# The last stage's output product in f16 halves: high and low parts of the mean, with the low part left in PSUM by a negated identity

## The chip, the cores and the metric

One Trainium2 chip, one NeuronCore. The metric is the device time of one execution of the program, in microseconds; of the kernel before, three runs are at hand. The shares of a stage come from one profiled execution.

## The reference

A graph network of two residual layers over 50,000 nodes with 256 features and 75,000 edges, sorted by destination. What the change touches is the end of the second layer, an attention over each node's edges with 8 heads:

```python
h = jnp.maximum(_layernorm(x, axis=-1), 0.0)
q = (h @ Wq + bq).reshape(n, DH, H) * scaling
k = (h @ Wk + bk).reshape(n, DH, H)
v = (h @ Wv + bv).reshape(n, DH, H)
s = jnp.einsum('edh,edh->eh', q[row], k[col])
m = jax.ops.segment_max(s, row, num_segments=n)
e = jnp.exp(s - m[row])
a = e / jax.ops.segment_sum(e, row, num_segments=n)[row]
out = jax.ops.segment_sum(a[:, None, :] * v[col], row, num_segments=n)
x = x + out.reshape(n, -1) @ Wo + bo
```

## The kernel before

The nodes stand in 98 tiles of 512 (128 partitions, 4 rows of nodes each: ROWS). The program runs through five parts, one after the other, which hand on tables in HBM and a few constants in SBUF: a preparation (weights, edges; line 388 and on), stage A (first layer's norm and product), stage B (second product and the sort of the edges), stage C (sums of neighbours, second norm, q, k and v; here v is written by `evacuate`, L1781, from a product in f16 parts at L1691), and stage E, the attention and the output product. The change is in stage E, with some constants made ready in the preparation and at the start of stage C.

Stage E is a pipeline written out by hand (`over_ring`): in one step every engine works on several tiles at once, `at(l)` being the tile that entered l steps ago. Six steps make one turn of a loop, so that a ring of six buffers has fixed addresses. Each engine has its own list for a step, taken strictly in order, and waits on semaphores:

- TensorE (`step` at L2180): turns the one-hot matrix of tile 0 (L2186) and counts its prefix (L2190); first half of the output product of tile 4 (`product`, L2154); first half of the mean of tile 3 (`mean(at(3), 0)`, L2166: four transposes, L2172, and the neighbours' share added, L2176); second half of the output product of tile 4; the edges' attention of tile 2 (L2202); second half of the mean of tile 3; q by edge for tile 0 (L2214); the scores laid out by node for tile 1 (L2223, into `e_small_ps`).
- VectorE (`step` at L2397): from that layout of tile 2 it masks (`e_seen`, L2328), takes peaks and differences, and while ScalarE takes the exponential does the products with k of tile 1 (L2344) and adds half a tile of output to x (`result`, L2314); then the attention of tile 2 is normalised (`e_attention`, L2360). It ends the step with scores, ranks, `e_of_edge` (L2391, which reads the same bank as L2223 writes) and the other half of `result`.
- ScalarE: copies (L2093 to L2102), the exponential (L2107), then for each of the two halves (kc) of the features a copy of the mean of tile 3 from PSUM (`e_mean_t`, L2118) and scalings of tile 2 by its attention (`e_mine`, L2126): 16 after the first copy and 8 after the second.
- GpSimd: scales the neighbours' v (L2065) and gathers rows (L2073).

The output product is in f32 and has, for each of 4 rows of a tile, one bf16 product for the bias (L2160) and two f32 products (L2162), each of which the profile shows as two MATMUL instructions:

```python
pe.wait_ge(mean_t_ready, t * 2 + 2)
for j in range(2):
    row = half * 2 + j
    nc.tensor.matmul(out_ps[:, j, :], all_b[:, :], b_out[:, :], start=True, stop=False)
    for kc in range(KC):
        last = nc.tensor.matmul(out_ps[:, j, :], mean_t[u][:, kc, row * P:(row + 1) * P],
                                w_out[:, kc, :], start=False, stop=kc == KC - 1)
```

## Time and profile before

| | us |
|---|---|
| median of 3 runs | 3436.98 |
| lowest and highest | 3434.53, 3438.17 |
| the profiled execution, its time | 3437.03 |
| the profiled execution, its span | 3435.2 |

The span is from the first to the last instruction of the trace. PE is TensorE's matmuls, PEld its weight loads (they run beside matmuls), DVE VectorE, ACT ScalarE, POOL GpSimd. A matmul's duration in the trace is longer than the distance to the next one's start, since matmuls are pipelined: rates are read from the starts. An idle time in brackets at the end of a timeline's row stands before that row, with what released it.

### The profile page before, as it was taken

To read this page: it belongs to the slowest core of one execution; us is meant where nothing else is said; L and a number is where in the kernel's file an instruction comes from. 1 tells how busy PE (TensorE), PEld (TensorE's weight loads), DVE (VectorE), ACT (ScalarE), POOL (GpSimd) and SP (SyncE) were. 2 spreads that over 40 slices of the span, in tenths; PEclk is the share of its full clock that TensorE was granted. 3 is DMA by queue.
4 is the path that set the end of the run, shared out by engine and by line. 5 is a ranking of instruction groups with operands and counts; after the bars stand their busy time and mean duration, and the time that the engine had idled before them with its cause. 6 is when DMAs were issued, how large, how long until landed. Compare 5 with 4: busy or idle time off the path is not lost. (4 is left out here: it accounts for less than half of the span.)

```text
span 3435.2 us, 80786 instructions
## 1 busy us (share of the span) xinstructions
PE 3089.9 (90%) x20244; PEld 2502.0 (73%) x20244; DVE 2812.0 (82%) x7373; ACT 2503.3 (73%) x7074; POOL 1953.9 (57%) x1668
## 2 busy tenths in 40 slices
PE   1699999699999569999999999994999999999999
PEld 0355555477776448888888888883899999999998
DVE  8788888578888358888888888885888888888887
ACT  0588888599997847777777777762777777777776
POOL 0344444045555277777777777763555555555553
PEclk6799999899999869999999999996999999999999
DMA  1355555388887658888888888875677777777774
GB/s 35 132 205 203 202 202 202 142 301 306 306 307 254 255 196 309 309 313 304 313 308 309 306 311 310 306 273 190 234 250 258 257 256 250 254 254 257 256 248 144
DMA packets 335629, 861.22 MB, mean 251 GB/s; under 512 B 98483, under 2 KB 152922, under 8 KB 323018
## 3 DMA queue, kind: packets, MB, share of 16 engines
q1 hardware_dynamic: 241082, 678.75, 55.2%
q0 software_dynamic: 66256, 78.94, 7.9%
q10 hardware_dynamic: 28224, 102.77, 7.4%
q8 instruction: 25, 0.41, 0.0%
q14 instruction: 42, 0.34, 0.0%
HBM read 521.95 MB, written 416.52 MB: 273 GB/s over the span
## 5 line engine op out<-in xcount | busy, mean ns | idle before, releaser
L1691 PE MATMUL c_qkv_ps<-w_qkv_hi,c_ht_hi 128*128 128x256 f16 x2352 | 642.0, 273 | 0.0
L1691 PE MATMUL c_qkv_ps<-w_qkv_lo,c_ht_hi 128*128 128x256 f16 x2352 | 642.0, 273 | 0.0
L1691 PE MATMUL c_qkv_ps<-w_qkv_hi,c_ht_lo 128*128 128x256 f16 x2352 | 642.0, 273 | 0.0
L2126 ACT ACTIVATE e_mine<-e_mine,e_attention 128x32 f32<-128x32 f32 x2352 | 518.7, 307 | 70.3 <-DVE e_attention L2360 70.3
L2073 POOL DMA_INDIRECT e_kv<-kv_table,e_near x392 | 402.1, 1026 | 113.1 <-issue 98.8
L1561 POOL DMA_INDIRECT c_got<-y_table,c_near x392 | 395.1, 1008 | 108.9 <-issue 98.0
L2162 PE MATMUL e_out_ps<-w_out,e_mean_t 128*128 128x256 f32 x1568 | 392.8, 380 | 0.0
L792 POOL DMA_INDIRECT dst_slots<-dst_word,dst_goal x240 | 236.9, 987 | 267.7 <-ACT a_hn L828 190.3
L862 PE MATMUL a_h_ps<-a_ht,w_t 128*128 128x512 f32 x784 | 361.1, 603 | 25.1 <-ACT h L810 21.5
L2065 POOL TENSOR_TENSOR e_kv<-e_kv,e_part_of 128x1024 f32<-128x1024 f32 x98 | 187.1, 1909 | 342.4 <-DVE e_part_of L2395 342.3
L1331 POOL DMA_INDIRECT src_slots<-staged_word,staged_goal x240 | 233.3, 972 | 250.8 <-DVE sort_lane_hot L1220 177.5
L1122 PE MATMUL mix_ps<-w_mix,hb 128*128 128x256 f32 x1568 | 358.0, 382 | 17.4 <-ACT hb L1091 17.4
L1122 PEld LDWEIGHTS mix_ps<-w_mix,hb 128*128 128x128 f32 x1568 | 296.9, 191 | 63.9 <-ACT hb L1091 21.5
L1554 POOL TENSOR_TENSOR c_x<-c_agg,c_x 128x1024 f32<-128x1024 f32 x98 | 231.2, 2359 | 127.6 <-ACT c_agg L1608 115.8
L2162 PEld LDWEIGHTS e_out_ps<-w_out,e_mean_t 128*128 128x128 f32 x1568 | 267.4, 191 | 44.0
L1678 PE MATMUL c_sum_ps<-c_got,c_sum_hot 128*128 128x256 f32 x784 | 218.8, 403 | 72.2 <-DVE c_agg L1802 48.1
L862 PEld LDWEIGHTS a_h_ps<-a_ht,w_t 128*128 128x128 f32 x784 | 141.6, 190 | 187.9 <-issue 187.9
L1619 ACT ACTIVATE c_hn<-c_x,c_shift,c_rstd 128x256 f32<-128x256 f32 x392 | 203.5, 590 | 95.7 <-DVE c_shift L1823 95.7
L1546 POOL TENSOR_TENSOR c_qk<-c_q,c_kv 128x1024 f32<-128x1024 f32 x98 | 232.5, 2373 | 34.8 <-DVE c_kv L1787 32.6
L1691 PEld LDWEIGHTS c_qkv_ps<-w_qkv_lo,c_ht_hi 128*128 128x128 f16 x2352 | 230.5, 98 | 27.0
L1691 PEld LDWEIGHTS c_qkv_ps<-w_qkv_hi,c_ht_lo 128*128 128x128 f16 x2352 | 230.5, 98 | 26.9
L1691 PEld LDWEIGHTS c_qkv_ps<-w_qkv_hi,c_ht_hi 128*128 128x128 f16 x2352 | 230.5, 98 | 24.7
(432 smaller groups left out, 7682.2 us busy)
## 6 DMA issues: line engine op xcount, KB each, us to landing
kv_table<-c_kv SPq DMA_DIRECT2D x98, 1024.0 KB, 6.7
h_table<-h ACTq DMA_DIRECT2D x98, 512.0 KB
h<-h_table SPq DMA_DIRECT2D x98, 512.0 KB
y_table<-y_out ACTq DMA_DIRECT2D x98, 512.0 KB
agg_table<-agg_out SPq DMA_DIRECT2D x98, 512.0 KB, 3.2
c_agg<-agg_table SPq DMA_DIRECT2D x98, 512.0 KB, 5.6
x_table<-c_x SPq DMA_DIRECT2D x98, 512.0 KB, 2.9
q_table<-c_q SPq DMA_DIRECT2D x98, 512.0 KB, 4.3
```

The costliest lines, as they stand in the source:

```text
L792: nc.gpsimd.indirect_dma_start(out=dst_slots, out_offset=bass.IndirectOffsetOnAxis(ap=dst_goal[:, k:k + 1], axis=0), in_=dst_word[:, k:k + ...
L862: last = nc.tensor.matmul(h1_ps[:, oc * TILE:(oc + 1) * TILE], w1_t[:, kc, oc * P:(oc + 1) * P], ht[u][:, kc, :], start=kc == 0, stop=kc = ...
L1122: last = nc.tensor.matmul(mix_ps[u][:, j * D:(j + 1) * D], hb[u][:, kc, j * P:(j + 1) * P], w_mix[:, kc, :], start=kc == 0, stop=kc == KC - 1)
L1331: nc.gpsimd.indirect_dma_start(out=src_slots, out_offset=bass.IndirectOffsetOnAxis(ap=staged_goal[h][:, k:k + 1], axis=0), in_=staged_word ...
L1546: nc.gpsimd.tensor_tensor(qk[u][:, :, :], qb[w][:, :, :], kv[w][:, :, 0, :], ALU.mult).then_inc(qk_ready, 1)
L1554: nc.gpsimd.tensor_tensor(x1[u][:, :, :], agg[w][:, :, :], xb[w][:, :, :], ALU.add).then_inc(x1_ready, 1)
L1561: nc.gpsimd.indirect_dma_start(out=got[w][:, j, :], out_offset=None, in_=y_table, in_offset=bass.IndirectOffsetOnAxis(ap=near[w][:, j:j + ...
L1678: last = nc.tensor.matmul(sum_ps[:, j * D:(j + 1) * D], sum_hot[w][:, row, :], got[w][:, row, :], start=True, stop=True)
L1691: last = nc.tensor.matmul(qkv_ps[n][:, j * D:(j + 1) * D], h[u][:, kc, j * P:(j + 1) * P], wt[:, kc, n * D:(n + 1) * D], start=m == 0, sto ...
L2073: nc.gpsimd.indirect_dma_start(out=kv[w][:, j, :], out_offset=None, in_=kv_table, in_offset=bass.IndirectOffsetOnAxis(ap=near[w][:, j:j + ...
L2126: last = nc.scalar.activation(of_head, of_head, ACT.Copy, scale=attention[u][:, j, h, 0:1])
L2162: last = nc.tensor.matmul(out_ps[:, j, :], mean_t[u][:, kc, row * P:(row + 1) * P], w_out[:, kc, :], start=False, stop=kc == KC - 1)
```

## The change

Stage E's output product takes f16 parts. The mean of tile 3 is copied by ScalarE from PSUM to f16 (`mean_hi`); TensorE adds to the same PSUM bank the product of a negated identity with `mean_hi` (`rest`), so that the bank holds what the f16 copy lacks; ScalarE copies that to f16 (`mean_lo`). The output product is then, for each half of the features, hi by hi, hi by lo and lo by hi, six f16 products in place of two f32 ones. The weights of the output are split once; they and v are scaled by powers of two, which `result` takes back.

```diff
@@ ScalarE, stage E
-                            nc.scalar.activation(mean_t[u][:, kc, :], mean_ps[kc][:, :], ACT.Copy).then_inc(mean_t_ready, 1)
+                            nc.scalar.activation(mean_hi[u][:, kc, :], mean_ps[kc][:, :], ACT.Copy).then_inc(mean_hi_ready, 1)
                         if at(2) is not None:
...
                             last.then_inc(own_shared, 1)
+                        if at(3) is not None:
+                            t, u = ring_tile(at(3)), at(3)[1] % 2
+                            act.wait_ge(rest_ready, t * 2 + (kc + 1))
+                            nc.scalar.activation(mean_lo[u][:, kc, :], mean_ps[kc][:, :], ACT.Copy).then_inc(mean_lo_ready, 1)
@@ TensorE, stage E
-                    pe.wait_ge(mean_t_ready, t * 2 + 2)
+                    pe.wait_ge(mean_lo_ready, t * 2 + 2)
...
-                        for kc in range(KC):
-                            last = nc.tensor.matmul(out_ps[:, j, :], mean_t[u][:, kc, row * P:(row + 1) * P],
-                                                    w_out[:, kc, :], start=False, stop=kc == KC - 1)
+                        passes = [(m, w, kc) for kc in range(KC)
+                                  for m, w in ((mean_hi, w_out_hi), (mean_hi, w_out_lo), (mean_lo, w_out_hi))]
+                        for k, (m, w, kc) in enumerate(passes):
+                            last = nc.tensor.matmul(out_ps[:, j, :], m[u][:, kc, row * P:(row + 1) * P],
+                                                    w[:, kc, :], start=False, stop=k == len(passes) - 1)
...
+                def rest(at, kc):
+                    t, u = ring_tile(at), at[1] % 2
+                    pe.wait_ge(mean_hi_ready, t * 2 + (kc + 1))
+                    nc.tensor.matmul(mean_ps[kc][:, :], minus_h[:, :], mean_hi[u][:, kc, :], start=False, stop=True,
+                                     skip_group_check=True).then_inc(rest_ready, 1)
...
                     if at(4) is not None:
                         product(at(4), 1)
+                    if at(3) is not None:
+                        rest(at(3), 0)
...
                             last.then_inc(q_ready, 1)
+                    if at(3) is not None:
+                        rest(at(3), 1)
                     if at(1) is not None:
@@ VectorE, stage E
-                    v.tensor_tensor(here, out_ps[:, :, :], here, ALU.add).then_inc(result_ready, 1)
+                    v.scalar_tensor_tensor(here, out_ps[:, :, :], out_unscale[:, 0:1], here, ALU.mult, ALU.add).then_inc(result_ready, 1)
@@ VectorE, stage C
-                    v.scalar_tensor_tensor(goes, qkv_ps[n][:, :].rearrange("p (j d) -> p j d", j=ROWS), unscale[:, 0:1],
+                    v.scalar_tensor_tensor(goes, qkv_ps[n][:, :].rearrange("p (j d) -> p j d", j=ROWS), (unscale_v if n == 2 else unscale)[:, 0:1],
@@ VectorE, start of stage C (before it: in the preparation, without the scaling by both_scale and the split of w_out)
+                v.tensor_scalar(b_out_n[:, :], b_out_n[:, :], both_scale[:, 0:1], None, ALU.mult)
+                chain(v.tensor_scalar(w_flat, w_flat, out_scale[:, 0:1], None, ALU.mult))
+                chain(v.tensor_copy(w_out_hi[:, :, :], w_out[:, :, :]))
+                chain(v.tensor_tensor(w_out_lo[:, :, :], w_out[:, :, :], w_out_hi[:, :, :], ALU.subtract))
...
@@ GpSimd, preparation
+                    pool.memset(minus_h[:, :], 0.0).then_inc(raising, 1)
+                    pool.wait_ge(raising, 3)
+                    pool.affine_select(out=minus_h[:, :], in_=minus_h[:, :], compare_op=ALU.not_equal, fill=-1.0, base=0,
+                                       pattern=[[-1, P]], channel_multiplier=1).then_inc(const_ready, 1)
...
+                    pool.wait_ge(o_peak_ready, 1)
+                    pool.partition_all_reduce(o_peaks[:, :], o_peak[:, :], P, bass.bass_isa.ReduceOp.max).then_inc(o_peaks_ready, 1)
```

In the preparation VectorE also takes the largest exponents of the output weights and of v's bias (three passes over 512 and two over 256 elements a partition) and makes the scales from them, some ten operations on one element a partition; the seven operations that split the output's bias into three bf16 rows move from there to the start of stage C. One semaphore of stage B, `agg_stored`, is now cleared with the others of its part.

The order of TensorE's work about the end of a step of stage E, in the kernel before (`e_mean_ps` is the mean of tile 3, `e_q_ps` q by edge, `e_small_ps` the scores laid out, `e_out_ps` the output product):

```order
L2176 MATMUL e_mean_ps<-e_hot,e_kv 128x128 x4
L2214 MATMUL e_q_ps<-e_q,e_hot_t 128x256 x4
L2223 MATMUL e_small_ps<-e_layered,e_hot 128x64 x4
L2186 MATMUL e_turn_ps<-ident_h,e_hot_h 128x128 x4
L2190 MATMUL e_prefix_ps<-e_hot_h,raised_h 128x128 x4
L2160 MATMUL e_out_ps<-b_out,all_b 128x256
L2162 MATMUL e_out_ps<-w_out,e_mean_t 128x256 x2
```

and after the change, at the same place:

```order
L2236 MATMUL e_mean_ps<-e_hot,e_kv 128x128 x4
L1389 ISA
L2276 MATMUL e_q_ps<-e_q,e_hot_t 128x256 x4
L2223 MATMUL e_mean_ps<-e_mean_hi,minus_h 128x512
L2287 MATMUL e_small_ps<-e_layered,e_hot 128x64 x4
L2243 REGISTER_ALU
L2246 MATMUL e_turn_ps<-ident_h,e_hot_h 128x128 x4
L2250 MATMUL e_prefix_ps<-e_hot_h,raised_h 128x128 x4
L2212 MATMUL e_out_ps<-b_out,all_b 128x256
L2216 MATMUL e_out_ps<-w_out_hi,e_mean_hi 128x256
L2216 MATMUL e_out_ps<-w_out_lo,e_mean_hi 128x256
```

One product over 512 columns, from `e_mean_hi`, stands between q and the layout of the scores.

ScalarE, from the first of the two copies of the mean to the end of the step, before:

```order
L2118 ACTIVATE e_mean_t<-e_mean_ps 128x512
L2126 ACTIVATE e_mine<-e_mine,e_attention 128x32 x16
L2117 REGISTER_ALU
L2118 ACTIVATE e_mean_t<-e_mean_ps 128x512
L2126 ACTIVATE e_mine<-e_mine,e_attention 128x32 x8
```

and after:

```order
L2166 ACTIVATE e_mean_hi<-e_mean_ps 128x512
L2174 ACTIVATE e_mine<-e_mine,e_attention 128x32 x16
L2179 ACTIVATE e_mean_lo<-e_mean_ps 128x512
L2165 REGISTER_ALU
L2166 ACTIVATE e_mean_hi<-e_mean_ps 128x512
L2174 ACTIVATE e_mine<-e_mine,e_attention 128x32 x8
L2179 ACTIVATE e_mean_lo<-e_mean_ps 128x512
```

The copy of the low part of the first half stands between the 16 scalings and the copy of the second half; the low part of the second half ends the step.

## Rows read from the trace of the kernel before

**Rows 1.** The page of the profile, busy time of each engine.

```profile
PE 3089.9 (90%) x20244; PEld 2502.0 (73%) x20244; DVE 2812.0 (82%) x7373; ACT 2503.3 (73%) x7074; POOL 1953.9 (57%) x1668
```

**Rows 2.** Busy time by window: stages C and E; PE, PEld, DVE, ACT, POOL, clock.

```profile
1400.00:2370.00 970.00, 907.62 (x7439) 789.62 (x7436) 818.06 (x1788) 684.21 (x1831) 719.40 (x489) 0.99 0.81 299
2428.00:3379.00 951.00, 950.99 (x6916) 867.26 (x6915) 849.66 (x1728) 727.02 (x2818) 547.13 (x455) 1.00 0.74 254
```

**Rows 3.** Groups by line, PE, window 2428:3379 (xcount | busy us, mean ns).

```profile
L2162 PE MATMUL e_out_ps<-w_out,e_mean_t 128*128 128x256 f32 x1456 | 364.7, 380 | 0.0
```

**Rows 4.** Timeline of PE, one step of stage E (start us, us, engine, line).

```profile
3002.99 1.00 PE L2223 MATMUL e_small_ps<-e_layered,e_hot 128*128 128x64 f32 x8
3003.83 0.39 PE L2186 MATMUL e_turn_ps<-ident_h,e_hot_h 128*128 128x128 f16 x4
...
3004.28 0.27 PE L2160 MATMUL e_out_ps<-b_out,all_b 128*128 128x256 bf16 x1
3004.38 1.03 PE L2162 MATMUL e_out_ps<-w_out,e_mean_t 128*128 128x256 f32 x4
3005.25 0.27 PE L2160 MATMUL e_out_ps<-b_out,all_b 128*128 128x256 bf16 x1
```

**Rows 5.** Timeline of DVE, the same step and the start of the next.

```profile
3004.17 0.42 DVE L2328 TENSOR_TENSOR e_seen<-e_small_ps,absent 128x256 f32<-128x256 f32 x1 [0.39 <-PE e_small_ps L2223]
...
3008.65 0.46 DVE L2360 TENSOR_TENSOR e_attention<-e_weight,e_inverse 128x288 f32<-128x288 f32 x1 [0.19 <-DVE e_inverse L2355]
...
3012.99 0.41 DVE L2391 TENSOR_TENSOR e_of_edge<-e_small_ps,e_layer 128x256 f32<-128x256 f32 x1
...
3014.80 0.42 DVE L2328 TENSOR_TENSOR e_seen<-e_small_ps,absent 128x256 f32<-128x256 f32 x1 [0.34 <-PE e_small_ps L2223]
```

**Rows 6.** Timeline of ACT, the same step.

```profile
3007.76 0.60 ACT L2118 ACTIVATE e_mean_t<-e_mean_ps 128x512 f32<-128x512 f32 x1 [1.39 <-PE e_mean_ps L2176]
3009.14 3.50 ACT L2126 ACTIVATE e_mine<-e_mine,e_attention 128x32 f32<-128x32 f32 x16 [0.79 <-DVE e_attention L2360]
3012.55 0.57 ACT L2118 ACTIVATE e_mean_t<-e_mean_ps 128x512 f32<-128x512 f32 x1
3013.03 1.80 ACT L2126 ACTIVATE e_mine<-e_mine,e_attention 128x32 f32<-128x32 f32 x8
```

**Rows 7.** Timelines of PE and DVE, a step that ends no turn of six.

```profile
2982.16 1.00 PE L2223 MATMUL e_small_ps<-e_layered,e_hot 128*128 128x64 f32 x8
...
2983.30 0.42 DVE L2328 TENSOR_TENSOR e_seen<-e_small_ps,absent 128x256 f32<-128x256 f32 x1 [0.46 <-PE e_small_ps L2223]
...
2987.69 0.46 DVE L2360 TENSOR_TENSOR e_attention<-e_weight,e_inverse 128x288 f32<-128x288 f32 x1 [0.19 <-DVE e_inverse L2355]
...
2991.77 0.42 DVE L2391 TENSOR_TENSOR e_of_edge<-e_small_ps,e_layer 128x256 f32<-128x256 f32 x1
```

**Rows 8.** Timelines of ACT and PE at the drain of stage E.

```profile
3409.39 0.57 ACT L2118 ACTIVATE e_mean_t<-e_mean_ps 128x512 f32<-128x512 f32 x1
...
3410.02 0.28 PE L2160 MATMUL e_out_ps<-b_out,all_b 128*128 128x256 bf16 x1 [0.29 <-ACT e_mean_t L2118]
```

**Rows 9.** One line of DVE: duration ns min/median/max, first and last start.

```profile
L2328 DVE TENSOR_TENSOR e_seen<-e_small_ps,absent x98: 423/425/425, 2398.4 to 3409.8; 128x256 f32<-128x256 f32 x98
```

**Rows 10.** Timeline of ACT in stage C, the copy to f16.

```profile
1395.24 0.58 ACT L1585 ACTIVATE c_ht_hi<-c_turn_ps 128x512 f16<-128x512 f32 x1
1395.71 0.71 ACT L1627 ACTIVATE c_sum_hot<-c_sum_hot,one_col 127x512 f32<-127x512 f32 x1
```

**Rows 11.** Timelines of DVE: start, end of preparation, start of stage C.

```profile
8.03 0.77 DVE L530 CAST edges_f<-edges 128x1176 f32<-128x1176 int32 x1 [8.03 <-POOL far_end L471]
...
90.44 0.28 DVE L669 CAST b_thirds<-b_out_n 128x256 bf16<-128x256 f32 x1
...
93.70 0.15 DVE L677 TENSOR_SCALAR unscale<-w_peaks 128x1 f32<-128x1 f32 x1
...
1224.15 0.69 DVE L1802 TENSOR_TENSOR c_agg<-c_sum_ps,c_agg 128x512 f32<-128x512 f32 x1 [15.55 <-PE c_sum_ps L1678]
```

More of the change, by code:

```diff
@@ L272, in build @@
         unscale = sb("unscale", [P, 1], where=early)
+        unscale_v = sb("unscale_v", [P, 1], where=early)
+        out_scale = sb("out_scale", [P, 1], where=early)
+        both_scale = sb("both_scale", [P, 1], where=early)
+        w_out = sb("w_out", [P, KC, D], where=early)
+        b_out_n = sb("b_out_n", [P, D], where=early)
         b_qkv = sb("b_qkv", [P, 3 * D], where=early)
@@ L383, in build @@
             n_loads = 14 + H
-            b_out_n = sb("b_out_n", [P, D], where=part)
-            b_rest = sb("b_rest", [P, 2, D], where=part)
-            b_thirds = sb("b_thirds", [P, 3, D], BF16, where=part)
+            o_power = sb("o_power", [P, KC * D], I32, where=part)
+            o_peak = sb("o_peak", [P, 1], where=part)
+            o_peaks = sb("o_peaks", [P, 1], where=part)
+            v_bias = sb("v_bias", [P, D], I32, where=part)
+            v_peak = sb("v_peak", [P, 1], where=part)
+            v_unscale = sb("v_unscale", [P, 1], where=part)
+            v_scale = sb("v_scale", [P, 1], where=part)
+            o_unscale = sb("o_unscale", [P, 1], where=part)
+            o_peak_ready = sem("o_peak_ready")
+            o_peaks_ready = sem("o_peaks_ready")
             with nc.Block() as block:
@@ L665, in _ @@
                     v.tensor_scalar(dst_goal[:, :], pair_f[:, 0, :], -float(subtiles), float(1 << 21), ALU.add, ALU.min)
-                    left = b_out_n[:, :]
-                    for third in range(3):
-                        link(v.tensor_copy(b_thirds[:, third, :], left))
-                        if third < 2:
-                            link(v.tensor_tensor(b_rest[:, third, :], left, b_thirds[:, third, :], ALU.subtract))
-                            left = b_rest[:, third, :]
-                    link(v.tensor_scalar(b_out[:, :], b_thirds[:, 0, :], ident[:, 0:1], None, ALU.mult))
-                    for third in (1, 2):
-                        link(v.scalar_tensor_tensor(b_out[:, :], b_thirds[:, third, :], ident[:, third:third + 1], b_out[:, :], ALU.mult, ALU.add))
                     dve.wait_ge(w_peaks_ready, 1)
@@ L971, in build @@
             y_stored = [sem(f"y_stored{u}") for u in two]
-            agg_stored = [pool_dma_sem(f"agg_stored{u}") for u in two]
+            agg_stored = [sem(f"agg_stored{u}") for u in two]
             own_scale = sb("own_scale", [P, NT * ROWS], where=part)
@@ L1459, in build @@
             not_slow = sb("c_not_slow", [P, 1], where=part)
+            b_rest = sb("b_rest", [P, 2, D], where=part)
+            b_thirds = sb("b_thirds", [P, 3, D], BF16, where=part)
             slots_loaded = sem("c_slots_loaded")
@@ L1777, in _ @@
                 v.scalar_tensor_tensor(slot_node[:, :], vacant[:, :], float(FAR), slots_f[:, 1, :], ALU.mult, ALU.add)
+                w_flat = w_out[:, :, :].rearrange("p k n -> p (k n)")
+                v.tensor_scalar(b_out_n[:, :], b_out_n[:, :], both_scale[:, 0:1], None, ALU.mult)
+                chain(v.tensor_scalar(w_flat, w_flat, out_scale[:, 0:1], None, ALU.mult))
+                chain(v.tensor_copy(w_out_hi[:, :, :], w_out[:, :, :]))
+                chain(v.tensor_tensor(w_out_lo[:, :, :], w_out[:, :, :], w_out_hi[:, :, :], ALU.subtract))
+                left = b_out_n[:, :]
+                for third in range(3):
+                    chain(v.tensor_copy(b_thirds[:, third, :], left))
+                    if third < 2:
+                        chain(v.tensor_tensor(b_rest[:, third, :], left, b_thirds[:, third, :], ALU.subtract))
+                        left = b_rest[:, third, :]
+                chain(v.tensor_scalar(b_out[:, :], b_thirds[:, 0, :], ident[:, 0:1], None, ALU.mult))
+                for third in (1, 2):
+                    chain(v.scalar_tensor_tensor(b_out[:, :], b_thirds[:, third, :], ident[:, third:third + 1], b_out[:, :], ALU.mult, ALU.add))
                 for l in range(LAYERS):
@@ L1931, in build @@
             part_of = [sb(f"e_part_of{w}", [P, ROWS, H], where=part) for w in short]
-            mean_t = [sb(f"e_mean_t{u}", [P, KC, TILE], where=part) for u in two]
+            mean_hi = [sb(f"e_mean_hi{u}", [P, KC, TILE], F16, where=part) for u in two]
+            mean_lo = [sb(f"e_mean_lo{u}", [P, KC, TILE], F16, where=part) for u in two]
             turn_ps = part.enter_context(nc.psum_tensor("e_turn_ps", [P, ROWS, 2 * P], F16))
```

31 lines of the change are left out of this document (26 added, 5 removed).

## The prediction

> **What bounds the kernel now.** The page first: PE is busy 90% of the span, VectorE 82%, ScalarE 73% [rows 1]. That is a mean over stages, so the busy times by window come next. From 2428 to 3379 us, in stage E, PE is busy for all of 951 us at a granted clock of 1.00 (2.4 GHz), its weight loads for 867, VectorE for 850, ScalarE for 727 [rows 2]. That stretch holds 1456 instructions of L2162 [rows 3], 16 to a tile, so 91 tiles; from tile to tile e_seen starts (3409.8 - 2398.4) / 97 = 10.43 us apart [rows 9]. Per tile VectorE works 9.3 us and ScalarE 8.0. The reader is to see two things in the timelines of one step. PE's rows follow each other without idle time [rows 4], while VectorE has 0.34 to 0.46 us of idle time before e_seen, released by PE [rows 5, 7], and ScalarE waits 1.39 us for the mean and 0.79 for the attention [rows 6]. So PE sets the pace, but VectorE's slack is small: in a step that ends a turn of six, from e_seen to e_seen are 10.63 us [rows 5], in which PE's L2223 waits for e_of_edge, since both use one bank.
>
> **What the change takes from PE.** A row of nodes now costs from L2160 to the next L2160 3005.25 - 3004.28 = 0.97 us [rows 4]. A product over 256 columns in 16 bits takes the distance from L2160 to L2162, 0.10 to 0.11 us; I take 0.109. With seven of them a row is 0.76, and four rows save 0.84 us per tile. The two new products over 512 columns cost twice that distance each, 0.22, so 0.44 for both. PE's work falls by 0.40 us, to about 10.05. Here lies the gain that the change could have, and it is hidden unless nothing else closes the circle first.
>
> **What it adds on ScalarE.** Two more copies of 128x512 from PSUM. Such a copy takes ScalarE 0.48 us until its next instruction starts, 3013.03 - 3012.55 [rows 6], and 0.57 us until it is done. One to f16 took the same in stage C, 0.58 with the next one 0.47 later [rows 10]. ScalarE's work rises to 8.0 + 0.96 = 9.0 us per tile, well below 10.4: by its sum there is room. What counts is the place: the first new copy stands behind the 16 scalings, ahead of the copy that `rest(at(3), 1)` on PE waits for, and behind that one on PE stands L2223, which VectorE waits for.
>
> **The circle that this closes.** The attention of tile 2 needs the scores that L2223 wrote at the end of the step before. The scalings need that attention, the copies stand behind the scalings, the new product needs the copy, and the next L2223 stands behind the product. All of it is within one step, so its length is a floor under the step. From the end of L2223 (3002.99 + 1.00) [rows 4] in order: to e_seen 0.18; to the end of e_attention, 3009.11 - 3004.17 = 4.94 [rows 5]; to the first scaling 0.03; sixteen scalings 3012.55 - 3009.14 = 3.41; the low copy of the first half 0.48; the high copy of the second half, to its end, 0.57 [rows 6]; from a copy's end to PE, 3410.02 - 3409.96 = 0.06 [rows 8]; the new product 0.22; L2223 to its end 1.00 [rows 4]. The sum is 10.89 us. In a step that ends no turn, the first two terms are 0.14 and 2988.15 - 2983.30 = 4.85 [rows 7], and the sum is 10.76. Five of the one to one of the other give 10.78. None of the terms has slack inside: VectorE's idle times in that stretch are the 0.19 before e_attention, which follow from its own chain.
>
> I take 10.84. Between VectorE and PE a wait is followed by 0.14 to 0.18 us [rows 5, 7] where ScalarE to PE took 0.06; the circle has new waits on both engines, and the difference of about 0.1 may be paid at one of them. With none of it paid, 10.76; with two paid in full, 11.0.
>
> A second circle goes over two steps. From the end of L2223 to the end of the high copy of the second half as above, but only 0.48 of it, then eight scalings (8 times 3.41 / 16 = 1.70), the low copy 0.57, and 0.06 to PE: 0.15 + 4.87 + 0.03 + 3.41 + 0.48 + 0.48 + 1.70 + 0.57 + 0.06 = 11.75 to the start of the output product. From there PE has its step but for the first two rows and L2223: 10.43 - 0.45 (3004.28 - 3003.83) - 0.84 (3003.83 - 3002.99) [rows 4] = 9.14, less 0.84, plus 0.22 for the first new product, and then 0.22 and 1.00. That is 21.5 us for two steps, 10.75 for one: just below the first circle, so PE will stand twice in a step, about 0.6 us before the output product and about 0.2 before the second new product.
>
> **The rest of the change.** `result` has an operation with one more multiplication on VectorE, with the same sizes; L2344, of that kind, ran between the same kinds of operands at the pace of `result`: nothing. In the preparation VectorE loses the 3.26 us of the bias's split (93.70 - 90.44) [rows 11] and gets five short passes and some ten operations of 0.15 each, which I price between 2.5 and 4: -1 to +1. GpSimd makes one more constant ahead of VectorE's first instruction, which waits for GpSimd until 8.03 [rows 11]: two small operations, under 1 us. Together +0.5. At the start of stage C VectorE gets the split and three passes over the weights, 5 to 6 us in all; the cover is its 15.55 us of idle time before the first c_agg, released by PE [rows 11]. Were that gone, 5 us would be added. In the drain, the last three tiles' output products wait for the copy already, as in the step of [rows 8]; a product and a copy more, 0.22 + 0.57 and what lies between, less two halves of the product that are 0.42 shorter: +1.
>
> **Sum.** 97 steps times (10.84 - 10.43) = +40, +0.5 and +1: +41.5 us on the profiled execution's 3437.03, so 3478.5. That execution is 0.05 us from the median of the three runs, so the median after is put at 3478 us. Slower or faster by less than 0.2% (7 us) is what a measurement of this kernel cannot tell from no change.
>
> **Rivals.**
>
> PE lightened and nothing in its way. If the low copy or the scalings cost the circle at least 0.6 us less than summed (the point from which this decides is a circle under 10.2), the floor is VectorE's: e_seen to the end of e_of_edge 2992.19 - 2983.30 = 8.89 [rows 7], 0.15 to PE, 1.00 for L2223, 0.14 back, 10.18; at the end of a turn 10.63 as now. The mean of 10.26 saves 0.17 times 97, 16 us: 3422 us. For it speaks that PE is the engine without idle time in [rows 2] and ScalarE has 2.4 us free; against it, that every term of the circle is a row. The Trainium skill, Perfetto Trace Analysis, "Identifying the Most-Contended Engine", says to find the engine with the highest occupancy and optimize it first. By that rule the change, which takes 0.40 us per tile from PE and adds to an engine with room, would end here, at a gain; the trace agrees that PE is the busiest and does not show that lightening it is paid out. 9%.
>
> The waits add up. The circle of two steps is within 0.1 us of the first. If PE comes late to the output product and the mean of the next half is then late for ScalarE as well, the two no longer overlap; half of the 0.6 us wait, paid on top of 0.41, would be +0.3 per tile more, 3508 us; a tenth to a half of it gives 3484 to 3508. 12%.
>
> The clock. PE gets idle times. In stage C it was busy 908 of 970 us at a granted clock of 0.99 [rows 2], and here it would be busy 10.05 of 10.84, 93%, in gaps under 1 us. The Trainium skill, TensorE: Matmul & The Clock Gate, "A second HAM failure mode: psum-queue depth-cycling", tells of a kernel whose short idles between groups of matmuls made the clock go to and fro. Should it fall to 1.2 GHz for a tenth of the stage, PE's 10.05 would become 20.1 there, and 9.7 steps of 9.3 us more give +90: 3570 us. 2%.
>
> No difference that can be measured: the circle is 0.3 shorter than summed, between the two. 4%.
>
> **How the numbers follow.** The forecast, a floor of 10.70 to 11.0 and so 3465 to 3493 us, has 73%. Faster by over 0.2% has the first rival's 9%, no difference 4%, slower the forecast, the added waits and the clock: 87%. The range leaves out the faster rival, the clock and the far half of the added waits: 3463 to 3500 us.
>
> **What would show it.** In the changed kernel's trace the distance of e_seen should be 10.75 to 10.95 us; PE should show idle time before the output product's L2160, released by ScalarE's low copy, and before the second product from e_mean_hi, released by the high copy; PE's busy share in stage E about 93% at a clock of 1.00; VectorE's idle time before e_seen 0.8 us or more. The prediction is wrong if PE has no idle time there, if a scaling starts later than 0.1 us after e_attention, or if e_attention itself is late because `result` or the exponential waits.

## The result, and the profile after

| | before | after |
|---|---|---|
| median, us | 3437.47 (4 runs of the same session) | 3483.81 (4 runs, 3481.78 to 3485.63) |
| the profiled execution, its span | 3435.2 | 3480.0 |
| ratio | | 1.0134, 95% interval 1.0120 to 1.0149 |

The change makes the kernel 46.3 us slower; the forecast was 3478 us and a range of 3463 to 3500. The profiled execution of after took 3481.78 us.

Busy time of each engine on the page, and further down the chain that ended last:

```profile
PE 3080.6 (89%) x21224; PEld 2477.8 (71%) x21224; DVE 2828.7 (81%) x7392; ACT 2583.4 (74%) x7270; POOL 1956.9 (56%) x1671
...
PE 12%; ACT 10%; DVE 7%; issue 3%; DVEq 0%; DMA 0%; POOL 0%; ACTq 0%; POOLq 0%
```

That chain is followed back from the last instruction, in shares of the span, and covers about a third of it. In the kernel before it lay on PE almost alone; now it passes through three engines:

```profile
PE 30%; DMA 1%; DVE 1%; issue 0%; ACT 0%; POOL 0%; POOLq 0%; SPq 0%; DVEq 0%; ACTq 0%
```

Busy time by window in stage E (PE, PEld, DVE, ACT, POOL, clock), the answer to [rows 2]:

```profile
2440.00:3390.00 950.00, 903.59 (x7503) 809.25 (x7502) 826.46 (x1658) 767.43 (x2873) 524.60 (x437) 1.00 0.71 244
```

PE is no longer busy all the time: 46 of 950 us are idle, at a granted clock of 1.00 as before. No engine is busy throughout, which points to a circle of waits. The busy shares of the page hide this, since 89% stands where 90% stood [rows 1].

The waits in stage E (idle engine, who released it: us in total, times, longest), window 2450 to 3400:

```profile
ACT e_mean_hi L2166 <- PE e_mean_ps L2236: 134.6, 87, 1.6
...
DVE e_seen L2392 <- PE e_small_ps L2287: 61.2, 87, 0.8
...
ACT e_mine L2174 <- DVE e_attention L2424: 46.3, 87, 0.6
PE e_out_ps L2212 <- ACT e_mean_lo L2179: 43.4, 88, 0.5
PEld e_mean_ps L2223 <- ACT e_mean_hi L2166: 38.1, 87, 0.5
```

Both waits that the prediction named on PE are there, once a step each: 0.5 us before the output product (L2212), released by the low copy (about 0.6 forecast), and 0.4 us in the weight load of the second new product (L2223), released by the high copy (about 0.2 forecast).

One step in three timelines (line numbers have moved: the layout of the scores, L2223 before, is L2287 now, and L2223 is the new product). VectorE:

```profile
3004.73 0.42 DVE L2392 TENSOR_TENSOR e_seen<-e_small_ps,absent 128x256 f32<-128x256 f32 x1 [0.76 <-PE e_small_ps L2287]
...
3007.28 0.75 DVE L2378 SCALAR_TENSOR_TENSOR e_x<-e_out_ps,out_unscale,e_x 128x512 f32<-128x512 f32 x1
...
3009.22 0.46 DVE L2424 TENSOR_TENSOR e_attention<-e_weight,e_inverse 128x288 f32<-128x288 f32 x1 [0.19 <-DVE e_inverse L2419]
...
3015.60 0.42 DVE L2392 TENSOR_TENSOR e_seen<-e_small_ps,absent 128x256 f32<-128x256 f32 x1 [0.78 <-PE e_small_ps L2287]
```

ScalarE:

```profile
3009.71 3.50 ACT L2174 ACTIVATE e_mine<-e_mine,e_attention 128x32 f32<-128x32 f32 x16 [0.51 <-DVE e_attention L2424]
3013.11 0.58 ACT L2179 ACTIVATE e_mean_lo<-e_mean_ps 128x512 f16<-128x512 f32 x1
3013.59 0.58 ACT L2166 ACTIVATE e_mean_hi<-e_mean_ps 128x512 f16<-128x512 f32 x1
```

PE:

```profile
3003.58 1.00 PE L2287 MATMUL e_small_ps<-e_layered,e_hot 128*128 128x64 f32 x8
...
3005.53 0.28 PE L2212 MATMUL e_out_ps<-b_out,all_b 128*128 128x256 bf16 x1 [0.50 <-ACT e_mean_lo L2179]
...
3008.40 0.27 PE L2212 MATMUL e_out_ps<-b_out,all_b 128*128 128x256 bf16 x1
...
3009.17 0.27 PE L2212 MATMUL e_out_ps<-b_out,all_b 128*128 128x256 bf16 x1
...
3014.23 0.39 PE L2223 MATMUL e_mean_ps<-e_mean_hi,minus_h 128*128 128x512 f16 x1
3014.45 1.00 PE L2287 MATMUL e_small_ps<-e_layered,e_hot 128*128 128x64 f32 x8
```

Read as the prediction's circle, from the end of L2287 at 3004.58: 0.15 to e_seen, 4.95 to the end of e_attention (3009.68), 0.03, scalings 3.40, low copy 0.48, high copy 0.58 to its end (3014.17), 0.06, new product 0.22, L2287 1.00. The sum is 10.87 us, and from e_seen to e_seen are 3015.60 - 3004.73 = 10.87. The circle has no slack: it is the step. This step ends no turn of six; the one that does takes 11.01 us, from 3026.50 to 3037.51. Both are 0.11 to 0.12 above the prediction's sums of 10.76 and 10.89.

Over the stage:

```profile
L2392 DVE TENSOR_TENSOR e_seen<-e_small_ps,absent x98: 423/424/426, 2394.5 to 3450.7; 128x256 f32<-128x256 f32 x98
```

(3450.7 - 2394.5) / 97 = 10.89 us a step, against 10.43 [rows 9]. Of the 44.8 us between the two spans, 44.8 lie between the first and the last e_seen (1056.2 - 1011.4); ahead of it after is 3.9 us earlier, and behind it 3.9 us longer.

### The profile page after: what moved, and what is told of

Same layout as the page of the kernel before. It is cut to its first block and busy times, and to the rows that moved or that the text cites. A ratio compares the mean times of both kernels' runs of the same rounds, so it can differ in the third digit from the quotient of the medians.

```text
span 3480.0 us, 83059 instructions
## 1 busy us (share of the span) xinstructions
PE 3080.6 (89%) x21224; PEld 2477.8 (71%) x21224; DVE 2828.7 (81%) x7392; ACT 2583.4 (74%) x7270; POOL 1956.9 (56%) x1671
## 5 line engine op out<-in xcount | busy, mean ns | idle before, releaser
L1592 POOL DMA_INDIRECT c_got<-y_table,c_near x392 | 402.2, 1026 | 108.4 <-issue 96.4
L1669 ACT ACTIVATE c_state<-c_raw,no_self,has_self 128x8 f32<-128x8 f32 x392 | 122.0, 381 | 155.8 <-DVE c_raw L1881 155.8
L857 ACT ACTIVATE a_hn<-a_x,a_shift,a_rstd 128x256 f32<-128x256 f32 x392 | 203.3, 589 | 45.1 <-DVE a_shift L193 45.1
```

The costliest lines, as they stand in the source:

```text
L1592: nc.gpsimd.indirect_dma_start(out=got[w][:, j, :], out_offset=None, in_=y_table, in_offset=bass.IndirectOffsetOnAxis(ap=near[w][:, j:j + ...
```

## Experiments

Three sets of four kernels. Times are compared with runs of the kernel before on the same chip. In the first and third sets it took 3437.8 and 3437.7 us, as here; in the second, on another chip, 3486.7 us.

| kernel | median, us | ratio to before, 95% | e_seen to e_seen, mean of 97, us |
|---|---|---|---|
| low0_later | 3482.80 | 1.0116 to 1.0147 | 10.863 |
| low1_sooner | 3480.15 | 1.0105 to 1.0136 | 10.851 |
| both_moved | 3440.82 | 1.0001 to 1.0020 | 10.494 |
| high_between | 3443.94 | 1.0009 to 1.0027 | 10.505 |
| plain_result | 3763.34 | 1.0774 to 1.0821 | 13.107 (other chip) |
| hi_only | 3675.54 | 1.0490 to 1.0555 | 12.412 (other chip) |
| before_two_copies | 3492.51 | 1.0007 to 1.0025 | 10.531 (other chip) |
| result_sooner | 3657.12 | 1.0482 to 1.0520 | 12.244 (other chip) |
| changed_again | 3485.49 | 1.0122 to 1.0153 | 10.873 |
| plain_result_2 | 3477.85 | 1.0098 to 1.0129 | 10.817 |
| hi_only_2 | 3477.34 | 1.0100 to 1.0131 | 10.864 |
| result_sooner_2 | 3441.38 | 1.0003 to 1.0021 | 10.471 |

The rival theories: ScalarE's added work costs by its sum; PE's wait for the low copy is the cost; PE's own work is the floor.

### low0_later: the first low copy out of the first circle

ScalarE's order for a step (high and low copies of the two halves, scalings):

```diff
-high 0, scalings 1-16, low 0, high 1, scalings 17-24, low 1
+high 0, scalings 1-16, high 1, low 0, scalings 17-24, low 1
```

> The changed kernel with ScalarE's low copy of the first half moved from ahead of the high copy of the second half to behind it; nothing else. Theory A (two circles, each a floor under the step): the first circle, from L2223 over e_seen, the attention, sixteen scalings and the two copies back to L2223, loses one copy's 0.48 us and falls from 10.89 to 10.41; the second, over two steps and the output product, keeps both copies and stands at about 10.75 to 10.84 per step. So the step shortens by 0.05 to 0.14 us and the time falls by 5 to 14 us from the changed kernel's, to 3470 to 3479 us, with PE's wait for the low copy before the output product as long as before or longer. Rival B (only the first circle counts): the step falls to the PE's or VectorE's own 10.4 and the time to 3437 us or below. Rival C (what counts is ScalarE's summed work, which is unchanged): 3484 us, no change.

Measured 3482.80 us, 1 us below after: theory A's gain of 5 to 14 us did not come, though 0.48 us left the first circle. Rival B is out; rival C, no change, fits this run alone. The timelines of PE, VectorE and ScalarE show what held the step:

```profile
3002.43 1.00 PE L2300 MATMUL e_small_ps<-e_layered,e_hot 128*128 128x64 f32 x8
...
3004.55 0.28 PE L2225 MATMUL e_out_ps<-b_out,all_b 128*128 128x256 bf16 x1 [0.68 <-ACT e_mean_lo L2172]
...
3013.29 1.00 PE L2300 MATMUL e_small_ps<-e_layered,e_hot 128*128 128x64 f32 x8
...
3015.42 0.28 PE L2225 MATMUL e_out_ps<-b_out,all_b 128*128 128x256 bf16 x1 [0.69 <-ACT e_mean_lo L2172]
```

```profile
3003.57 0.42 DVE L2405 TENSOR_TENSOR e_seen<-e_small_ps,absent 128x256 f32<-128x256 f32 x1 [0.57 <-PE e_small_ps L2300]
...
3004.90 1.28 DVE L2421 SCALAR_TENSOR_TENSOR e_qk<-e_q_ps,e_kv 128x512 f32<-128x512 f32 x2
3006.30 0.75 DVE L2391 SCALAR_TENSOR_TENSOR e_x<-e_out_ps,out_unscale,e_x 128x512 f32<-128x512 f32 x1
...
3008.24 0.46 DVE L2437 TENSOR_TENSOR e_attention<-e_weight,e_inverse 128x288 f32<-128x288 f32 x1 [0.19 <-DVE e_inverse L2432]
```

```profile
3008.73 3.50 ACT L2183 ACTIVATE e_mine<-e_mine,e_attention 128x32 f32<-128x32 f32 x16 [0.51 <-DVE e_attention L2437]
3012.14 0.57 ACT L2166 ACTIVATE e_mean_hi<-e_mean_ps 128x512 f16<-128x512 f32 x1
3012.62 0.57 ACT L2172 ACTIVATE e_mean_lo<-e_mean_ps 128x512 f16<-128x512 f32 x1
3013.09 1.79 ACT L2183 ACTIVATE e_mine<-e_mine,e_attention 128x32 f32<-128x32 f32 x8
3014.79 0.57 ACT L2172 ACTIVATE e_mean_lo<-e_mean_ps 128x512 f16<-128x512 f32 x1
```

The prediction's circle over two steps comes near, but has slack. From L2300's end at 3003.43 to the output product at 3015.42 are 11.99 us, and from the output product to the end of the next L2300, 3014.29 - 3004.55, 9.74; the prediction had 11.75 and 9.74. But 0.20 us of the 11.99 are a wait inside it: `result` (L2391) starts 1.40 us after the start of the two products with k, where 1.20 is the distance without a wait. Without it the two steps are 21.53, or 10.77 for one, and the step is 10.86.

What sets the step is a shorter circle, which the prediction did not have. It is closed within one step and does not pass through L2300: the output product of tile 4 is needed by `result`, which stands on VectorE ahead of the attention of tile 2; the scalings need that attention, all copies stand behind the first sixteen of them, and the next output product needs the last low copy. From the output product at 3004.55: 1.75 to `result`, 2.40 to the end of e_attention, 0.03, scalings 3.41, copies 0.48 and 0.47, scalings 1.70, the last low copy 0.57 to its end, 0.06 to the next output product. The sum is 10.87, which is the whole distance 3015.42 - 3004.55. The move of the first low copy leaves this circle as long as it was. In the changed kernel it is as long as the first one: from the output product to `result` are 1.75 us there too, and the output products of the steps at 3005.53 and 3016.40 are 10.87 apart. So two circles stand at the same length in the changed kernel, and low0_later cuts only one.

### low1_sooner: the second low copy ahead of the last scalings

```diff
-high 0, scalings 1-16, low 0, high 1, scalings 17-24, low 1
+high 0, scalings 1-16, low 0, high 1, low 1, scalings 17-24
```

> The changed kernel with ScalarE's low copy of the second half moved from behind the last eight scalings to ahead of them; nothing else. Theory A: this takes the eight scalings, 1.7 us, out of the circle over two steps and leaves the first circle, 10.89 us, as it is, so the distance between two e_seen stays 10.85 to 10.93 us and the time within 4 us of the changed kernel's 3484, while PE's wait before the output product (43.4 us over 88 steps) shrinks to nearly nothing and its wait before the second new product grows. Rival B (the wait for the low copy before the output product, about 0.5 us a step, is what the change costs): the time falls by 20 to 40 us. Rival C (ScalarE's sum): no change, and the waits stay where they are.

Measured 3480.15 us and 10.85 us a step, at the edge of A's 4 us: the first circle still stands. The waits, window 2450 to 3400:

```profile
DVE e_seen L2405 <- PE e_small_ps L2300: 61.6, 88, 0.8
PEld e_mean_ps L2236 <- ACT e_mean_hi L2166: 57.9, 88, 0.7
...
PE e_out_ps L2225 <- DVE e_x L2391: 23.3, 87, 0.3
```

The row "PE e_out_ps <- ACT e_mean_lo", 43.4 us in after, is gone, and 3.7 us of time went with it; the wait for the high copy grew from 38.1 to 57.9 instead. The circle through `result` lost 1.70 us, and the first circle alone holds the step. So PE's largest visible wait was by itself worth under 4 us, and rival B falls.

### both_moved: both circles cut

```diff
-high 0, scalings 1-16, low 0, high 1, scalings 17-24, low 1
+high 0, scalings 1-16, high 1, low 0, low 1, scalings 17-24
```

> The changed kernel with ScalarE's order: high copy of half one, sixteen scalings, high copy of half two, both low copies, eight scalings. Same instructions, same sums. Theory A: both circles are cut, the first to 10.41 us, the second below it, so the step is 10.41 to 10.48 us and the time 3436 to 3444 us: all of the change's loss is given back by the order alone. Rival C (ScalarE's added work or the two extra hand-overs cost what was lost, wherever they stand): 3475 to 3484 us. Rival D (PE is bound by its own work again): with PE at 10.05 a step it would be faster than the kernel before, 3400 to 3425 us; A says that this gain stays out.

Measured 3440.82 us: 43 of the 46 us are given back by the order of ScalarE's list, with every instruction of the change in place. Rival C falls with it. Either half alone gave 1 to 4 us, both together 43; that is what two circles of one length do. The step of 10.494 us is just above A's 10.41 to 10.48. Rival D falls too: PE's work is below the kernel before's and is not paid out. Busy time in stage E:

```profile
2440.00:3390.00 950.00, 924.11 (x7771) 839.21 (x7770) 857.57 (x1719) 806.91 (x2986) 536.83 (x447) 1.00 0.73 251
```

PE idles 26 us there, and every engine has room. PE's timeline of a step that ends a turn shows one wait, for the first half of `result`:

```profile
3001.72 1.02 PE L2300 MATMUL e_small_ps<-e_layered,e_hot 128*128 128x64 f32 x8
...
3006.34 0.28 PE L2225 MATMUL e_out_ps<-b_out,all_b 128*128 128x256 bf16 x1 [0.28 <-DVE e_x L2391]
```

### high_between: more slack in both circles

```diff
-high 0, scalings 1-16, high 1, low 0, low 1, scalings 17-24
+high 0, scalings 1-12, high 1, low 0, scalings 13-16, low 1, scalings 17-24
```

> The changed kernel with ScalarE's order: high copy of half one, twelve scalings, high copy of half two, low copy of half one, four scalings, low copy of half two, eight scalings. Same instructions. Theory A: four scalings, 0.85 us, and a copy, 0.48, are out of the first circle (9.56 us left); the circle over two steps comes to about 10.4, and VectorE's own floor is 10.2 in a step that ends no turn and 10.63 in one that does, 10.26 to 10.35 in the mean. So the step is 10.3 to 10.45 us and the time 3425 to 3440 us, equal to the kernel before or up to 12 us below it. Rival C (ScalarE's sum): 3475 to 3484 us. Rival D (PE's own 10.05 is the only floor left): 3400 us.

Measured 3443.94 us, 4 us above A's range, and 10.505 us a step, as in both_moved. A further 0.85 us off the first circle brings nothing, so another chain holds the step at 10.50, above the 10.26 that I had put as VectorE's floor. The wait in the row above gave the next candidate: L2300, e_seen, the products with k, `result`, the second half of the output product (one PSUM bank serves both halves), and PE's list on to L2300.

### result_sooner and result_sooner_2: that candidate cut

```diff
-products q times k 0 and 1, result 0
+product q times k 0, result 0, product q times k 1
```

> The kernel with the high copy of half two between the scalings, and in it VectorE's `result` of the first half moved from behind the second product q times k to between the two. Its reason: in both kernels with ScalarE's order changed the step is 10.50 us, not the 10.3 to 10.4 hoped for, and PE stands 0.28 us a step before the second half of the output product, released by `result`. That is a third circle: L2300's end, 0.15 to e_seen, 3.35 to the end of `result`, 0.06, then PE without idle time for 6.0 and L2300 again, 10.42 to 10.70. Theory A: the move takes 0.6 us out of it, and the step falls to VectorE's floor, 10.25 in a step that ends no turn and 10.65 to 10.70 in one that does, 10.33 in the mean; the time is 3420 to 3432 us, 6 to 17 us below the kernel before and about 16 below the run without the move. Rival (PE's wait for `result` is made up elsewhere, or another chain stands just below 10.5): 3438 to 3444 us.

> As in the first try, for a chip on which the step keeps its pace. Theory A: without the third circle the step is VectorE's floor, and the shortest steps of the first try, 10.34 and 10.42 in steps that end no turn, 10.56 and 10.67 at a turn, give 10.40 to 10.45 in the mean: 97 times 0.06 to 0.10 us, 6 to 10 us, below the runs without the move (3441 and 3444 us), so 3430 to 3437 us, equal to the kernel before or just below. Rival: 3440 to 3444 us, if PE's wait for `result` only moves on.

On the chip of the third set 3441.38 us, and 10.47 us a step against 10.49 and 10.51: 0.6 us out of that circle gave at most 0.03, and the rival is right. PE's timeline:

```profile
3004.80 1.08 PE L2301 MATMUL e_small_ps<-e_layered,e_hot 128*128 128x64 f32 x8
...
3011.11 1.10 PE L2278 MATMUL e_small_ps<-e_attention,e_hot_t 128*128 128x64 f32 x8 [0.19 <-DVE e_attention L2438]
...
3015.50 1.07 PE L2301 MATMUL e_small_ps<-e_layered,e_hot 128*128 128x64 f32 x8
```

PE's wait for `result` is gone, and it waits for e_attention instead: from L2301's end at 3005.88 to L2278 at 3011.11 are 5.23 us of VectorE's chain, and from there to L2301's end at 3016.57 5.46 us of PE's own list, together 10.69 in this step, which ends a turn. This further circle holds VectorE's chain and half of PE's list and nothing of ScalarE's copies. It is read from rows of one kind of step; no run cut it, so that it sets the pace is not shown. No version here beats the kernel before.

### plain_result and plain_result_2: the price of `result`

The kernel leaves out the scaling back of the output product:

```diff
-v.scalar_tensor_tensor(here, out_ps[:, :, :], out_unscale[:, 0:1], here, ALU.mult, ALU.add)
+v.tensor_tensor(here, out_ps[:, :, :], here, ALU.add)
```

> The changed kernel with `result` as the plain addition of the kernel before; it leaves out the scaling back of the output product by out_unscale. In the changed kernel's trace this operation takes 0.74 us, before it took 0.68, and it stands once inside the first circle, between e_seen and e_attention, which the prediction priced at nothing. Theory A: the first circle falls by 0.07 us, from 10.89 to 10.82, and the time by 97 times 0.07 = 7 us, to 3474 to 3480 us. Rival: `result` is hidden beside ScalarE's exponential and costs nothing: 3482 to 3485 us.

> As in the first try (the scaling back by out_unscale is left out), for a chip on which the step keeps its pace. Theory A: `result` at 0.68 instead of 0.74 us shortens the first circle by 0.07 us, steps of 10.82 instead of 10.89, and 4 to 9 us off the changed kernel of this set. Rival: nothing off. On a chip as in the set before, only the undisturbed steps can be read: 10.78 to 10.80 in a step that ends no turn, instead of 10.86.

VectorE's timeline in result_sooner_2 has two operations of one size side by side, a product with k, which multiplies by a constant and then by a tensor, and `result`, which multiplies by a factor per partition and then adds:

```profile
3007.47 0.68 DVE L2422 SCALAR_TENSOR_TENSOR e_qk<-e_q_ps,e_kv 128x512 f32<-128x512 f32 x1
3008.07 0.74 DVE L2392 SCALAR_TENSOR_TENSOR e_x<-e_out_ps,out_unscale,e_x 128x512 f32<-128x512 f32 x1
```

In the third set plain_result took 3477.85 us against 3485.49 of changed_again, 7.6 us less, and 10.817 against 10.873 us a step, 97 times 0.056 = 5.4 us of it in the steps. Theory A holds. That `result` takes longer than the product with k may come from the factor or from the second operation; no run separates them. The second set's run of it is told below.

### hi_only and hi_only_2: a third of the output product

The kernel leaves out the two passes with low parts:

```diff
-((mean_hi, w_out_hi), (mean_hi, w_out_lo), (mean_lo, w_out_hi))
+((mean_hi, w_out_hi),)
```

> The changed kernel with the output product's two passes by low parts left out, 16 of 24 products over 256 columns per tile, so its output has the high parts' product alone; both copies, both new products and all waits stay. PE's work falls by 16 times 0.109 = 1.75 us per tile, to about 8.3. Theory A (the first circle sets the step, and the output product is not in it): the distance between two e_seen stays 10.85 to 10.91 us and the time 3478 to 3486 us. Rival D (PE's work sets the pace, as its 95% busy share in stage E of the changed kernel would suggest): the step falls by up to 1.75 us to VectorE's floor near 10.3, time 3420 to 3440 us. Between them: if the circle over two steps were what binds, half of 1.75 would come off, and the next floor, the first circle, would stop it.

> As in the first try (two of three passes of the output product are left out), for a chip on which the step keeps its pace. Theory A: steps stay at 10.84 to 10.91 us and the time within 6 us of the changed kernel of this set. In the first try, on the slower chip, the shortest steps came in rows of 10.84 to 10.93 us with PE at its full pace, which already speaks for it. Rival D (PE's work counts): 3420 to 3440 us where the changed kernel takes 3484.

In the third set, with 1.75 us less of PE's work per tile:

```profile
2440.00:3390.00 950.00, 789.09 (x6104) 665.62 (x6103) 825.93 (x1660) 768.19 (x2875) 520.78 (x438) 1.00 0.71 244
```

and the row of e_seen (first and last start):

```profile
L2392 DVE TENSOR_TENSOR e_seen<-e_small_ps,absent x98: 423/425/426, 2394.8 to 3448.6; 128x256 f32<-128x256 f32 x98
```

PE is busy 83% instead of 95%, and the step stays (3448.6 - 2394.8) / 97 = 10.86 us. Removing 170 us of PE's work (97 times 1.75) took 8 us off the time (2 us outside A's bound of 6), of which 5 lie behind the last e_seen: 3475.5 - 3448.6 = 26.9 us, against 31.9 in changed_again. This is the plainest evidence that PE's work does not set the pace of the changed kernel.

### before_two_copies: ScalarE's added work alone

Kernel before, at the end of each half's scalings:

```diff
+if at(3) is not None:
+    nc.scalar.activation(again[at(3)[1] % 2][:, kc, :], w_out[:, :, :].rearrange("p k n -> p (k n)"), ACT.Copy)
```

> The kernel before with two copies of 128x512 f32 to f16 per step on ScalarE, at the places of the two low copies, from a constant into a buffer that nobody reads; nothing waits for them, and they wait for nothing. ScalarE's sum is then that of the changed kernel, 9.0 us per tile, and the first circle of the kernel before, which has no product behind the copy of the second half, is lengthened only as far as the mean of the second half is late for PE. Theory A: PE keeps the pace, 10.43 to 10.46 us a step and 3434 to 3441 us, no change. Rival C (the two copies cost by ScalarE's time alone): 3460 to 3484 us. Half open: the output product needs both halves of the mean; should it wait, PE's own work of 10.43 leaves it no slack and every wait is paid in full, 3441 to 3455 us.

Measured on the second set's chip, 3492.51 us against 3486.7 of the kernel before there, 1.0016 (1.0007 to 1.0025). Busy time from 2600 us on, and e_seen from 2800 to 3350 us:

```profile
2600.00:3390.00 790.00, 789.61 (x5732) 718.12 (x5731) 706.30 (x1432) 667.43 (x2489) 452.40 (x378) 1.00 0.74 254
```

```profile
L2331 DVE TENSOR_TENSOR e_seen<-e_small_ps,absent x52: 424/425/426, 2806.2 to 3339.6; 128x256 f32<-128x256 f32 x52
```

and in the kernel before:

```profile
L2328 DVE TENSOR_TENSOR e_seen<-e_small_ps,absent x53: 423/425/425, 2805.5 to 3349.3; 128x256 f32<-128x256 f32 x53
```

(3339.6 - 2806.2) / 51 = 10.46 us, and (3349.3 - 2805.5) / 52 = 10.46 us: in these steps the two copies cost nothing, though ScalarE is busy 84% instead of 76%. Rival C falls a second time. Over the whole stage the distance is 10.53 us against 10.43: of the 10.1 us between 1021.5 and 1011.4, 7.4 lie in the first two steps (27.6 us against 20.2 in the kernel before), where PE is not yet busy all the time. Whether the copies or the chip did that is open, since no trace of the kernel before was taken on that chip.

### changed_again, and the chip of the second set

> The changed kernel itself, unaltered, beside the three runs that follow, since the set before ran on a chip on which the kernel before took 3487 us and kernels whose PE waits for other engines in each step took 3657 to 3763 us, in steps of 10.6 to 16 us. If this set runs on such a chip: theory A with the clock (idle time of PE inside each step lets its pace fall there) expects 3650 to 3780 us for the changed kernel, against 3475 to 3490 us on the first chip; the rival, that something particular to those four runs slowed them, expects 1.0134 times the kernel before, 3533 us. If it runs on a chip where the kernel before takes 3437 us: 3480 to 3486 us.

On the third set's chip the changed kernel took 3485.49 us, 1.0137 (1.0122 to 1.0153): the first result again. The three kernels of the second set that were run again show that it was not the kernels alone; the set ran on another chip and at another time, which no run separates:

| kernel | second set: us, clock in 2440 to 3390 | third set |
|---|---|---|
| plain_result | 3763.34, 0.96 | 3477.85, 1.00 |
| hi_only | 3675.54, 0.90 | 3477.34, 1.00 |
| result_sooner | 3657.12, 0.95 | 3441.38, 1.00 |

In the same set before_two_copies, whose PE is busy throughout from 2600 us on, held 10.46 us a step there at 1.00. Nor is it that one chip alone: in the first set one of the eleven executions of both_moved took 3702.11 us, at a granted clock of 0.827 over the whole program where the others had 0.96. PE's busy time and clock in result_sooner, two us at a time:

```profile
2790.00:2792.00 2.00, 2.00 (x21) 1.00 0.97 311
2792.00:2794.00 2.00, 0.88 (x8) 1.00 1.01 269
2794.00:2796.00 2.00, 0.00 (x0) 1.00 1.01 399
2796.00:2798.00 2.00, 1.17 (x6) 0.64 0.59 226
2798.00:2800.00 2.00, 2.00 (x11) 0.51 0.00 0
```

and the first half of `result` in the same step, on VectorE:

```profile
2795.93 0.75 DVE L2392 SCALAR_TENSOR_TENSOR e_x<-e_out_ps,out_unscale,e_x 128x512 f32<-128x512 f32 x1 [4.19 <-remote]
```

PE's rows show no work for 3.96 us before 2796.83, and the clock fell to the lower level of 1.2 GHz before that work began; the products over 256 columns then start 0.21 us apart instead of 0.11. But `result` was already 4.2 us late for a product whose rows end before 2792 at a clock of 1.00. Either PE was slower there than its rows say or something else held it: that is open. So is how much of the time each of the two cost; the mean clock does not say it, since plain_result was the slowest of the three at the highest, 0.96. The Trainium skill, TensorE: Matmul & The Clock Gate, "A second HAM failure mode: psum-queue depth-cycling", tells of short idles between groups of matmuls that make the clock go to and fro. By that rule a kernel with a wait on PE in each step would be slower than its circle says; the second set's trace agrees in that the clock goes to and fro, though the idle time above is 3.96 us and not a short one, and that of after, at 1.00 with PE idle 46 of 950 us, does not agree. How the changed kernel itself runs on that chip was not tried.

## Why the prediction was right, by its steps

**PE's gain.** Right in size by the rows: a row of nodes takes 0.77 us from L2212 to L2212 (0.76 forecast) and a new product 0.22. Right that it is not paid out, even in both_moved.

**ScalarE's place, not its sum.** Right: before_two_copies (nothing for 0.96 us a step of added work) against both_moved (43 us for the same instructions in another order).

**The first circle.** Right as the mechanism. Summed 10.76 (10.78 with the turns), taken 10.84, measured 10.89. The terms of ScalarE and PE are within 0.01 us in the step shown. Its marks were there, too: both waits on PE, and 0.76 us of idle time before e_seen (0.8 forecast); PE's share was 95% where 93% was forecast. The missing 0.11 us are on VectorE, between e_seen and the end of e_attention: 4.95 us in the step shown, 4.85 in the kernel before [rows 7], of whose step these are the rows of the two products with k and of `result`:

```profile
2984.62 1.28 DVE L2344 SCALAR_TENSOR_TENSOR e_qk<-e_q_ps,e_kv 128x512 f32<-128x512 f32 x2
2985.82 0.68 DVE L2314 TENSOR_TENSOR e_x<-e_out_ps,e_x 128x512 f32<-128x512 f32 x1
```

From the start of `result` to the end of e_attention were 2.33 us and are 2.40. `result` was priced at "nothing", from a row of the same operation with a constant factor; with a factor per partition it takes 0.75 us, and it lies inside the circle: plain_result_2 puts it at 0.056 us a step, 5 to 8 us. Ahead of `result` 1.20 us have become 1.23, which fits its wait for the later output product, as the rows of low0_later do, where the product is later still and the distance 1.40. And the 0.06 added "for waits" was not paid: ScalarE to PE took 0.06 and PE to VectorE 0.15, the values of the rows. That this allowance covered half of what was missing is luck; without it the forecast would have been 3472 us, still in its range. A price read off the nearest row needs the row's operations and operand kinds, too; an allowance without a mechanism hid that this was missing.

**The second circle.** Put at 10.75, "just below the first". As summed it is right: low0_later has 10.77 without the wait inside it. What the prediction missed is the shorter circle through `result`, which stands at 10.87, as long as the first: it gave `result` no place between the output product and the attention. This changed little in the forecast, but it is why low0_later gained 1 us and not 5 to 14.

**The rest.** Preparation and start of stage C, +0.5 forecast: the first e_seen came 3.9 us earlier in the first trace and 1.3 earlier in changed_again, so no cost of this part shows; in the traces of the first and third sets the first e_seen lies anywhere from 2393 to 2400 us. The drain, +1 forecast, became 3.9 us in the first trace and 6.5 in changed_again (31.9 against 25.4). Steps +40, measured 44.8.

**The rivals.** PE lightened and nothing in its way, 3422 us, was wrong twice: the circle stood in the way, and its floor, VectorE's 10.26, is too low. With ScalarE out of the way the step is 10.47 to 10.51, held, as the rows read, by circles through VectorE and PE together. The Trainium skill, Perfetto Trace Analysis, "Identifying the Most-Contended Engine", says to optimize the engine with the highest occupancy first, and to judge TensorE's headroom by its weight loads. Before the change PE is that engine by either, with 951 and 867 us against VectorE's 850 [rows 2]; the traces of after and both_moved, with less work on PE and no gain, do not bear the rule out here, and hi_only_2, with PE 83% busy, has no gain in the step over the changed kernel either. "The waits add up" reaches down to the measured time, but not by its mechanism: low1_sooner removed PE's wait for the low copy and 4 us at most went with it. The clock stayed at 1.00 in stage E in the traces of the first result and of the first and third sets, and all eight executions of the changed kernel ran at one pace. The second set, and one execution of both_moved in the first, show that kernels close to it do lose their clock, which the one trace that the 2% was taken from could not tell.

## What to carry to other kernels

When every engine has idle time in each step, write down the circles of waits that return to the same instruction and sum each; the busiest engine's share says nothing about which is longest, and two circles of equal length must both be cut before anything is gained. An operation added to an engine with room costs by its place in that engine's list: put what others wait for ahead of what nobody waits for. A lighter busiest engine pays only down to the next circle, and here that was at the old pace already.

## What the runs showed of the hardware that was not expected

- The same three kernels took 3441 to 3478 us on one chip and 3657 to 3763 us in a set on another, on which the kernel before took 3487 instead of 3437. The slow ones were those whose PE waits in each step, at a granted clock of 0.90 to 0.96 in stage E; before_two_copies, whose PE does not, stayed within 0.2% of the kernel before.
- VectorE's multiply and add from PSUM over 128x512 took 0.74 to 0.75 us with a factor per partition, where a multiply and multiply with a constant factor (the products with k) took 0.68; the plain addition in its place took 0.056 us less of each step.
- An idle time of 161 us in 950 on PE (hi_only_2) left the granted clock at 1.00 on the third set's chip.
